# Sum passes by pairs of chunks, and the opening's loads issued inside the sort, in a four-layer graph network

## The chip, the cores and the metric

The kernel runs on one core of a Trainium2 chip. The metric is the device time of one execution in microseconds (us); less is better. The engines are named as in the profile: PE (TensorE, with PEld for its weight loads), DVE (VectorE), ACT (ScalarE), POOL (GpSimd) and SP (SyncE, which only issues DMAs).

## The reference, cut to what matters

There are 3125 nodes of 256 features and 100000 edges (`src`, `dst`), and four layers. Each layer has a graph part, a mixing part and experts. The change touches the graph sums of layers 1 and 2 and the ordering of edges in front of layer 0.

```python
# layer 1: mean over the edges of one source and one type, then a product with weights
index = row * N_EDGE_TYPE + edge_type              # row = src, col = dst, 7 types
sums = segment_sum(x[col], index)                  # 3125 * 7 segments
mean = sums / maximum(segment_sum(1, index), 1)
out  = mean.reshape(n, -1) @ weights
# layer 2: weighted sum over the edges of one destination
norm = dinv[row] * ew * dinv[col]
out  = segment_sum((x @ W)[row] * norm[:, None], col)
```

The kernel multiplies first and sums afterwards: for layer 1 it stores a table `rel_table` with a row of 256 numbers per node and type, and adds to each source node the rows of its edges, each weighted with one over the size of its run of equal source and type. For layer 2 the table `el` has one row per node, weighted with the edge weight.

## The kernel before, in words

**Order of the edges.** `order_edges` (line 2921) builds constants, stores a record of four numbers per edge (`store_records`), and sorts the edges twice, by destination (`order_by_dst`, line 508) and by source (`order_by_src`, line 451). Every stage is a `phase` (line 83): it has its own semaphores, and at its end all engines meet at a barrier. So a stage lasts as long as its last engine, SP's issuing included.

`order_by_dst` begins with the stage `dst_keys` (lines 518 to 537): SP issues the load of `dst`, then the loads in `ahead` (lines 522 and 523), which are the 17 weights, biases and gains that the opening of layer 0 reads and the two halves of x; GpSimd writes edge numbers and VectorE packs keys. `build_sort` (line 193) then sorts 128 x 1024 keys: exchanges on VectorE, with TensorE transposes and copies on ScalarE and VectorE from level 11 on; SP has nothing in it. `build_chunk_order` turns the keys to chunks of 128 edges. There are 784 chunks (CHUNKS_S), the last of them with padding.

`build_unit_tiles` (line 401) groups the chunks by G = 4 to 196 units and finds for each the tile of 125 nodes (25 tiles) in which its first node lies. Where a unit goes across the border of two tiles, its sum must reach both: so 24 further units are appended (UNITS_S = 220 in all, 880 chunks), each a copy of the unit at one border. The copies are made in a loop of 24 turns on VectorE: `value_load` of the position, then one copy for each name in `o["copied"]` (lines 440 to 444); line 447 subtracts each unit's first node. For the source order this is the stage `src_tiles`, for the destination order `dst_tiles`.

**Record gathers.** After the destination order is known, GpSimd fetches the 784 chunks' records by indirect DMAs (line 561), one per chunk. `SHARES` (line 41) divides them over the stages of the source order: 14 in `src_keys`, 280 in the sort, 40 in `runs`, 8 in `src_chunks`, 10 in `src_parts`, 36 in `src_tiles`, 16 in `src_out`, in which SP stores the source order to four DRAM arrays (node, row, w, tile) for layer 1. The other 380 are fetched in the opening of layer 0 (`open0`, line 1592), the first 128 of them paced. `unpack_records` (line 570) waits for all of them before layer 0 goes on.

**Sum passes.** `build_sums` (line 592) serves layer 1 (`layer1`, line 2966) and layer 2 (`layer2`, line 2975). For each of 220 units
- GpSimd gathers 4 chunks of 128 rows into one of 10 lanes (line 609), after the unit that had the lane is summed;
- VectorE makes four one-hot matrices (chunk edge by node of the tile, times the weight, line 622) in one of 14 buffers;
- TensorE multiplies the four with the rows into one PSUM slot of 16 (line 648). fp32 gives two PE instructions per matmul;
- VectorE loads the unit's tile to a register and adds the slot to the accumulator of that tile (line 631), BEHIND = 10 units after the one-hots.

TensorE signals once in BATCH = 4 units, on `batch_summed`. GpSimd's lanes, VectorE's one-hot buffers and VectorE's additions all wait on that semaphore:

```python
def batches_of(u):
    return u // BATCH + 1
# GpSimd, unit u, before its four gathers
if u >= LANES_S:
    pool.wait_ge(s["batch_summed"], batches_of(u - LANES_S))
```

TensorE waits for unit u on `step` u + 1, which VectorE raises after its one-hots of unit u and its addition of unit u - 10.

Of the kernel before, what the change touches and what calls it, by code (L numbers as in the profile page):

```python
# [6 lines left out]
F32 = mybir.dt.float32  # L7
# [25 lines left out]
LANES_S = 10  # L33
BATCH = 4
HOTS_S = 14
SLOTS_S = 16
BEHIND = 10
# [3 lines left out]
SHARES = (14, 280, 40, 8, 10, 36, 16)  # L41
# [151 lines left out]
def build_sort(nc, c, tag, T, turned, pool_work=None):  # L193
# [10 lines left out]
    with phase(nc, tag, "ready", "turned", "moved", "chain") as s, nc.Block() as block:  # L204
        @block.tensor
# [245 lines left out]
def order_by_src(nc, c, I, o, pool_works):  # L451
# [3 lines left out]
    o["copied"] = ("node", "row", "w")  # L455
    with ExitStack() as ctx:
# [48 lines left out]
        build_unit_tiles(nc, c, "src_tiles", o, pool_works[5])  # L505


def order_by_dst(nc, c, I, o, ahead):
# [4 lines left out]
    with ExitStack() as ctx:  # L513
# [24 lines left out]
        build_sort(nc, c, "dst_sort", T, turned)  # L538
# [48 lines left out]
def batches_of(u):  # L587

    return u // BATCH + 1


def build_sums(nc, c, tag, table, o, w, acc):

    assert UNITS_S % BATCH == 0 and HOTS_S >= BEHIND + BATCH and SLOTS_S >= BEHIND + BATCH and BATCH % 2 == 0
    with ExitStack() as ctx:
        rows = [ctx.enter_context(nc.sbuf_tensor(f"{tag}_rows{l}", [P, G, D], F32)) for l in range(LANES_S)]
        hot = [ctx.enter_context(nc.sbuf_tensor(f"{tag}_hot{l}", [P, G, R], F32)) for l in range(HOTS_S)]
        banks = [ctx.enter_context(nc.psum_tensor(f"{tag}_sum{l}", [R, 2, D], F32)) for l in range(SLOTS_S // 2)]
        slot = lambda u: banks[u % SLOTS_S // 2][:, u % 2, :]
        with phase(nc, tag, "cleared", "batch_summed", "step", *[f"rows_in{l}" for l in range(LANES_S)]) as s, nc.Block() as block:  # L600
            @block.gpsimd
            def _(pool):
                for u in range(UNITS_S):
# [3 lines left out]
                    for g in range(G):  # L607
                        k = u * G + g
                        nc.gpsimd.indirect_dma_start(rows[l][:, g, :], None, table, bass.IndirectOffsetOnAxis(ap=o["row"][:, k:k + 1], axis=0)  # L609
                                                     ).then_inc(s[f"rows_in{l}"], 16)  # L610

            @block.vector
            def _(dve):
                v = nc.vector
                v.memset(acc[:], 0.0).then_inc(s["cleared"], 1)

                def make_hot(u):
                    if u >= HOTS_S:
                        dve.wait_ge(s["batch_summed"], batches_of(u - HOTS_S))
                    for g in range(G):  # L620
                        k = u * G + g
                        last = v.tensor_scalar(hot[u % HOTS_S][:, g, :], c["iota"][:, 0:R], o["node"][:, k:k + 1], w[:, k:k + 1], ALU.is_equal, ALU.mult)
                    return last

                def add(u, steps):
                    at = dve.value_load(o["tile"][0:1, u:u + 1], min_val=0, max_val=TILES - 1)
                    to = acc[:, bass.ds(at, 1), :].rearrange("p t d -> p (t d)")
                    if u % BATCH == 0:
                        dve.wait_ge(s["batch_summed"], batches_of(u))
                    dve.wait_ge(s["step"], steps)  # L630
                    return v.tensor_tensor(to, to, slot(u), ALU.add)  # L631

                dve.wait_ge(s["cleared"], 1)
                for n in range(UNITS_S + BEHIND):
                    if n < UNITS_S:
                        last = make_hot(n)
                    if n >= BEHIND:
                        last = add(n - BEHIND, n)
                    last.then_inc(s["step"], 1)

            @block.tensor
            def _(pe):
                for u in range(UNITS_S):
                    l = u % LANES_S
                    pe.wait_ge(s["step"], u + 1)
                    pe.wait_ge(s[f"rows_in{l}"], 16 * G * (u // LANES_S + 1))
                    for g in range(G):
                        last = nc.tensor.matmul(slot(u), hot[u % HOTS_S][:, g, :], rows[l][:, g, :], start=(g == 0), stop=(g == G - 1))  # L648
                    if u % BATCH == BATCH - 1:
                        last.then_inc(s["batch_summed"], 1)  # L650
# [2262 lines left out]
def alloc_order(nc, ctx, by, names):  # L2913

    sb = lambda n, sh, d=F32: ctx.enter_context(nc.sbuf_tensor(f"{by}_order_{n}", sh, d))
    o = {n: sb(n, [P, COLS_S], I32 if n == "row" else F32) for n in names}
    o["tile"], o["again"] = sb("tile", [P, UNITS_S], I32), sb("again", [P, TILES], I32)
    return o


def order_edges(nc, c, I, by_src, by_dst, ahead):
# [4 lines left out]
    order_by_src(nc, c, I, by_src, [record_share(nc, by_dst, n) for n in range(6)])  # L2926
# [39 lines left out]
def layer1(nc, c, m, I, dram, by_src):  # L2966

    open1(nc, c, m, I, dram)
    with nc.sbuf_tensor("gnn1_acc", [R, TILES, D], F32) as acc:
        build_sums(nc, c, "sum1", dram["rel_table"], by_src, by_src["w"][:], acc)  # L2970
# [4 lines left out]
def layer2(nc, c, m, I, dram, by_dst):  # L2975

    with ExitStack() as ctx:
# [15 lines left out]
        with nc.sbuf_tensor("gnn2_acc", [R, TILES, D], F32) as acc:  # L2993
            build_sums(nc, c, "sum2", dram["el"], by_dst, by_dst["record"][:, :, 1], acc)
# [380 lines left out]
```

## Time and profile before

| what | us |
|---|---|
| median of the runs (lowest to highest) | 10286.64 (10276.81 to 10286.82) |
| the profiled execution, its own time | 10346.27 |
| its span, first to last instruction | 10344.1 |
| first sum pass, first to last gather | 3691.1 to 4935.2 |
| second sum pass, first to last gather | 5480.8 to 6724.9 |

The mean granted clock of TensorE is 0.80. In the profile a busy time is the time in which an engine works on instructions with data; register operations, such as those of `value_load`, semaphores and the issuing of DMAs are not in it. A row of the timeline has the start, the length, the engine, the line and what it writes and reads; in brackets stands how long the engine was idle before, and what is held to have ended that. The name of a releaser is inferred and can be wrong where several semaphores are waited for.

### The profile page before, as it was taken

What the parts mean: (1) busy time and instruction counts of PE and PEld (TensorE: products, weight loads), DVE (VectorE), ACT (ScalarE), POOL (GpSimd) and SP (SyncE); (2) the same over time, 40 slices, a digit from 0 to 9 for tenths busy, and PEclk for the clock granted to TensorE, in tenths of its full rate; (3) what the DMA queues carried; (4) which work ended last, traced back from release to release, by engine and by line L of the source; (5) the groups of instructions that cost most, each with busy time, mean ns of one, the idle gap of its engine ahead of it and who ended that gap; (6) DMA issues with size and microseconds to landing.
All of it is one profiled execution on the core that took longest, in us unless ns stands there. A gap on an engine that the chain in (4) does not pass through costs nothing. (4 is left out here: it accounts for less than half of the span.)

```text
span 10344.1 us, 95778 instructions
## 1 busy us (share of the span) xinstructions
PE 6288.6 (61%) x28050; PEld 4786.2 (46%) x28050; DVE 4856.2 (47%) x13537; ACT 2032.4 (20%) x5038; POOL 4487.0 (43%) x4412
## 2 busy tenths in 40 slices
PE   0001305999996864454754444553955788887699
PEld 0000204888874533333543333342853677775466
DVE  5644515888874632222242222274123566666633
ACT  0000102444442300000120000012212232222322
POOL 0375675666650046666005666602021666664000
PEclk9999657999997976666776666675987777777799
DMA  1000002333320133333002333302861232332000
GB/s 33 6 2 7 11 4 83 83 83 83 83 74 12 63 103 92 94 92 92 23 14 81 92 92 94 92 7 59 308 205 30 75 80 79 81 81 60 11 13 19
DMA packets 404431, 697.45 MB, mean 67 GB/s; under 512 B 154143, under 2 KB 267784, under 8 KB 403421
## 3 DMA queue, kind: packets, MB, share of 16 engines
q0 software_dynamic: 206848, 480.68, 17.2%
q1 hardware_dynamic: 197076, 210.68, 6.4%
q8 instruction: 236, 3.87, 0.2%
q14 instruction: 271, 2.22, 0.1%
HBM read 631.46 MB, written 59.47 MB: 67 GB/s over the span
## 5 line engine op out<-in xcount | busy, mean ns | idle before, releaser
L648 PE MATMUL sum_sum<-sum_rows,sum_hot 128*125 128x256 f32 x3520 | 1233.9, 489 | 1284.1 <-issue 802.1
L665 POOL DMA_INDIRECT att_rows<-el_table,dst_order_row x1520 | 1590.0, 1046 | 950.6 <-issue 388.4
L648 PEld LDWEIGHTS sum_sum<-sum_rows,sum_hot 128*125 128x125 f32 x3520 | 828.9, 241 | 1689.3 <-issue 1538.5
L609 POOL DMA_INDIRECT sum_rows<-rel_table,src_order_row x880 | 834.9, 949 | 1038.3 <-ACTq L600 628.2
L609 POOL DMA_INDIRECT sum_rows<-el_table,dst_order_row x880 | 834.7, 948 | 955.1 <-ACTq L600 544.7
L561 POOL DMA_INDIRECT dst_order_record<-records,dst_order_row x784 | 835.2, 1065 | 679.6 <-PEq L461 363.2
L631 DVE TENSOR_TENSOR gnn_acc<-gnn_acc,sum_sum 125x256 f32 x440 | 180.5, 410 | 1887.7 <-DMA ffn1e_w<-in_L_ffn_W_dram 938.6
L1143 PE MATMUL att_sum<-att_rows,att_hot 128*125 128x265 f32 x1280 | 426.8, 489 | 47.2 <-ACT att_part L1210 39.9
L665 POOL DMA_INDIRECT dst_order_record<-el_table,dst_order_row x240 | 268.5, 1119 | 407.2 <-SPq L967 241.7
L807 PE MATMUL att_found<-gnn_to_dst,att_hot_t 125*128 x1760 | 439.5, 393 | 2.5 <-ACT att_hot_t L856 2.5
L831 PE MATMUL att_sum<-att_rows,att_hot 128*125 128x261 f32 x1760 | 427.7, 385 | 2.4 <-ACT att_rows L869 2.4
L869 ACT ACTIVATE att_rows<-att_rows,att_p 128x257 f32<-128x257 f32 x880 | 375.7, 498 | 0.0
L797 PE MATMUL att_turn_p<-ident,att_hot 128*125 128x128 f32 x880 | 155.1, 299 | 328.0 <-DVE att_hot L675 315.4
L1143 PEld LDWEIGHTS att_sum<-att_rows,att_hot 128*125 128x125 f32 x1280 | 291.7, 240 | 126.4 <-issue 59.4
L1108 PEld LDWEIGHTS att_found<-layer_a_dst,att_hot_t 125*128 125x128 f32 x1760 | 275.0, 226 | 162.2 <-issue 141.0
L807 PEld LDWEIGHTS att_found<-gnn_to_dst,att_hot_t 125*128 125x128 f32 x1760 | 320.8, 192 | 38.4 <-issue 3.2
L831 PEld LDWEIGHTS att_sum<-att_rows,att_hot 128*125 128x125 f32 x1760 | 314.2, 188 | 47.8 <-ACT att_rows L869 2.5
L1108 PE MATMUL att_found<-layer_a_dst,att_hot_t 125*128 x1760 | 253.3, 267 | 122.9 <-issue 69.4
L751 DVE CUSTOM_DVE_ANT_0 att_high<-att_high,att_att 128x256 f32<-128x256 f32 x880 | 319.9, 418 | 0.0
L1169 ACT COPY att_hot_t<-att_turn_p 125x512 f32<-125x512 f32 x220 | 129.4, 588 | 793.2 <-PE att_turn_p L1098 447.8
L797 PEld LDWEIGHTS att_turn_p<-ident,att_hot 128*125 128x125 f32 x880 | 113.5, 188 | 369.8 <-DVE att_hot L675 367.2
L211 PE MATMUL src_order_turned<-ident,src_order_keys 128*128 128x128 f32 x112 | 27.6, 428 | 417.8 <-DVE src_order_keys L242 320.5
(775 smaller groups left out, 12991.9 us busy)
## 6 DMA issues: line engine op xcount, KB each, us to landing
block_w<-in_L_ffn_W_dram SPq DMA_DIRECT2D x112, 512.0 KB, 6.3
block_w<-in_L_ffn_W_dram SPq DMA_DIRECT2D x56, 1024.0 KB
att_rows<-el_table,dst_order_row POOLq DMA_INDIRECT x1520
rel_table<-open_st SPq DMA_DIRECT2D x25, 784.0 KB
sum_rows<-rel_table,src_order_row POOLq DMA_INDIRECT x880
sum_rows<-el_table,dst_order_row POOLq DMA_INDIRECT x880
dst_order_record<-records,dst_order_row POOLq DMA_INDIRECT x784
pairs<-zeros SPq DMA_DIRECT2D x1, 7168.0 KB
```

Of the source, the lines that this page charges most:

```text
L561: nc.gpsimd.indirect_dma_start(o["record"][:, k, :], None, o["records"], bass.IndirectOffsetOnAxis(ap=o["row"][:, k:k + 1], axis=0)).then_ ...
L609: nc.gpsimd.indirect_dma_start(rows[l][:, g, :], None, table, bass.IndirectOffsetOnAxis(ap=o["row"][:, k:k + 1], axis=0)).then_inc(s[f"row ...
L631: return v.tensor_tensor(to, to, slot(u), ALU.add)
L648: last = nc.tensor.matmul(slot(u), hot[u % HOTS_S][:, g, :], rows[l][:, g, :], start=(g == 0), stop=(g == G - 1))
L665: nc.gpsimd.indirect_dma_start(rows[l][:, g, 0:width], None, table, bass.IndirectOffsetOnAxis(ap=o["row"][:, k:k + 1], axis=0)).then_inc(s ...
L751: last = v.tensor_tensor_reduce(high[:, g, :], high[:, g, :], att[:], 0.8, 0.0, ALU.mult, ALU.add, score[u % 2][:, g:g + 1])
L797: last = t.transpose(turn_p[:, g * P:(g + 1) * P], hot[u % HOTS][:, g, :], c["ident"][:])
L807: last = t.matmul(found[:, g, :], hot_t[u % TURNED][:, g * P:(g + 1) * P], nodes_of_unit(to_dst, tile), start=True, stop=True)
L831: last = t.matmul(sums[u % 2][:, 0:S], hot[u % HOTS][:, g, :], rows[u % LANES_A][:, g, :], start=(g == 0), stop=(g == G - 1))
L869: last = a.activation(own_rows[:, g, 0:D + 1], own_rows[:, g, 0:D + 1], ACT.Copy, scale=p[u % 2][:, g:g + 1])
L1108: done = t.matmul(found[u % 2][:, g, 0:H], hot_t[u % 2][:, g * P:(g + 1) * P], nodes_of_unit(to_dst, tile), start=True, stop=True)
L1143: done = t.matmul(sums[u % SUMS_B][:, 0:W + 1], hot[u % HOTS_B][:, g, :], rows[u % LANES_B][:, g, :], start=(g == 0), stop=(g == G - 1))
```

## The change

The constants: LANES_S 10 to 9, HOTS_S 14 to 10, BEHIND 10 to 6, BATCH goes; HALF_S = 2, MAIN_S = 782, EXTRA_S = 48, SUM_COLS = 830, SUM_UNITS = 208, SUMS_S = 415. SHARES becomes (14, 280, 40, 8, 10, 8): 360 gathers before the opening of layer 0 and 424 in it.

In the sum passes a sum and a tile now belong to two chunks (HALF_S), 415 of them; at each of the 24 borders two chunks are repeated instead of four. Of 784 chunks 782 are used: 100000 edges fill 781.25. Rows are still gathered, one-hot made and multiplied by units of four chunks, 208 of them. TensorE signals each unit (`summed`), VectorE its one-hots (`hot`) and each addition (`added`). The tiles and the repeated chunks are now worked out at the head of each pass (`prepare_sums`), from the plain order; the stage `src_tiles` goes, and the fourth store and load (tile) with it. `dst_tiles` remains, since layers 0 and 3 use its units; for layer 2 node numbers are rebuilt from it.

```diff
-def build_sort(nc, c, tag, T, turned, pool_work=None):
+def build_sort(nc, c, tag, T, turned, pool_work=None, ahead=None):
...
+        @block.sync
+        def _(sp):
+            if ahead:
+                for to, frm in ahead[1]:
+                    sp.dma_start(to, frm).then_inc(ahead[0], 16)
@@ order_by_src
-        build_unit_tiles(nc, c, "src_tiles", o, pool_works[5])
@@ order_by_dst
                 sp.dma_start(dst_i[:], as_chunks(I["dst"])).then_inc(s["loaded"], 16)
-                for to, frm in ahead[1]:
-                    sp.dma_start(to, frm).then_inc(ahead[0], 16)
...
-        build_sort(nc, c, "dst_sort", T, turned)
+        build_sort(nc, c, "dst_sort", T, turned, ahead=ahead)
@@ new, called first by VectorE's part of build_sums
+def prepare_sums(nc, c, dve, pe_done, to_pe, own, b, node, tile_of, row, w):
...
+    if tile_of is None:
+        own(v.tensor_copy(b["node"][:, main], node[:, main]))
+    else:
+        own(v.tensor_copy(b["tile"][:, 0:UNITS_1], tile_of[:, 0:UNITS_1]))
+        own(v.scalar_tensor_tensor(b["node"][:, 0:CHUNKS_S]..., col_of(b["tile"][:, 0:UNITS_1], G), float(R), node[:, 0:CHUNKS_S]..., ALU.mult, ALU.add))
+    own(v.tensor_copy(b["w"][:, main], w[:, main]))
+    v.tensor_copy(b["tile"][:, extras], c["iota"][:, 1:TILES]).then_inc(to_pe, 1)
+    dve.wait_ge(pe_done, 1)
+    own(v.tensor_scalar(b["tile"][:, halves], b["first_p"][:, 0:MAIN_S // HALF_S], -62.0, 1.0 / R, ALU.add, ALU.mult))
+    own(v.tensor_scalar(b["tile"][:, halves], b["tile"][:, halves], 8388608.0 * 1.5, -8388608.0 * 1.5, ALU.add, ALU.add))
+    own(v.tensor_scalar(b["less"], b["tile"][0:R, halves], c["part"][0:R], 0.5, ALU.subtract, ALU.is_lt))
+    own(v.tensor_reduce(b["cnt"][:], b["less"], AX, ALU.add))
...
+    for k in range(TILES - 1):
+        at = dve.value_load(b["again"][0:1, k:k + 1], min_val=0, max_val=MAIN_S - HALF_S)
+        to = MAIN_S + k * HALF_S
+        v.tensor_copy(b["node"][:, to:to + HALF_S], b["node"][:, bass.ds(at, HALF_S)])
+        v.tensor_copy(b["w"][:, to:to + HALF_S], b["w"][:, bass.ds(at, HALF_S)])
+        last = v.tensor_copy(b["row"][:, to - MAIN_S:to - MAIN_S + HALF_S], row[:, bass.ds(at, HALF_S)])
+    own(last)
+    own(v.tensor_tensor(b["node"]..., b["node"]..., col_of(b["tile"][:], HALF_S), ALU.subtract))
@@ build_sums, GpSimd
+                for u in range(SUM_UNITS):
                     l = u % LANES_S
                     if u >= LANES_S:
-                        pool.wait_ge(s["batch_summed"], batches_of(u - LANES_S))
+                        pool.wait_ge(s["summed"], u - LANES_S + 1)
...
+                            if k == MAIN_S:
+                                pool.wait_ge(s["cleared"], 1)
@@ build_sums, VectorE
+                prepare_sums(nc, c, dve, s["firsts"], s["ready"], own, b, node, tile_of, row, w)
                 v.memset(acc[:], 0.0).then_inc(s["cleared"], 1)
...
                     if u >= HOTS_S:
-                        dve.wait_ge(s["batch_summed"], batches_of(u - HOTS_S))
+                        dve.wait_ge(s["summed"], u - HOTS_S + 1)
...
+                    last.then_inc(s["hot"], 1)
+                def add(u):
+                    for h in range(u * G // HALF_S, ends(u)):
+                        at = dve.value_load(b["tile_i"][0:1, h:h + 1], min_val=0, max_val=TILES - 1)
+                        to = acc[:, bass.ds(at, 1), :].rearrange("p t d -> p (t d)")
+                        if h == u * G // HALF_S:
+                            dve.wait_ge(s["summed"], u + 1)
+                        if h:
+                            dve.wait_ge(s["added"], h)
+                        v.tensor_tensor(to, to, slot(h), ALU.add).then_inc(s["added"], 1)
@@ build_sums, TensorE
+                pe.wait_ge(s["ready"], 1)
...
+                last.then_inc(s["firsts"], 1)
+                pe.wait_ge(s["ready"], 2)
+                nc.tensor.matmul(b["again_p"], c["ones"][0:R, :], b["spread"][:], start=True, stop=True).then_inc(s["firsts"], 1)
+                for u in range(SUM_UNITS):
                     l = u % LANES_S
-                    pe.wait_ge(s["step"], u + 1)
+                    pe.wait_ge(s["hot"], u + 1)
+                    if u >= slots_ahead:
+                        pe.wait_ge(s["added"], ends(u - slots_ahead))
...
+                    for k in chunks(u):
+                        last = nc.tensor.matmul(slot(k // HALF_S), hot[u % HOTS_S][:, k % G, :], rows[l][:, k % G, :], start=(k % HALF_S == 0), stop=(k % HALF_S == HALF_S - 1))
+                    last.then_inc(s["summed"], 1)
```

The tables in DRAM and the source order's arrays get 784 columns instead of 880.

## Rows read from the trace of the kernel before

**Rows 1.** The page: its first line, and part 1 (busy us, share, instructions).

```profile
span 10344.1 us, 95778 instructions
...
PE 6288.6 (61%) x28050; PEld 4786.2 (46%) x28050; DVE 4856.2 (47%) x13537; ACT 2032.4 (20%) x5038; POOL 4487.0 (43%) x4412
...
```

**Rows 2.** Timeline of the opening: start, us, engine, line, idle before.

```profile
...
37.03 0.36 SPq L523 DMA_DIRECT2D open_w_el<-in_L_gnn_W_src_dram  x1
...
43.45 0.99 DVE L537 TENSOR_TENSOR dst_order_keys<-dst_order_dst_i,dst_order_edge_i 125x800 int32<-125x800 int32 x1
...
83.53 26.42 SPq L523 DMA_DIRECT2D X<-in_x_dram  x2
...
110.89 0.43 DVE L253 TENSOR_SCALAR dst_order_keys<-dst_order_keys 128x512 f32<-128x512 f32 x1 [66.45 <-PEq L88]
...
```

**Rows 3.** Timeline of VectorE in the source order's last stages.

```profile
...
905.32 0.97 DVE L503 SCALAR_TENSOR_TENSOR src_order_typ<-src_order_dst,src_order_typ 128x784 f32<-128x784 f32 x1
...
931.75 0.17 DVE L444 COPY src_order_node<-src_order_node 128x4 f32 x1 [0.77 <-DVE src_order_tile L439]
...
938.99 0.17 DVE L444 COPY src_order_node<-src_order_node 128x4 f32 x1 [0.78 <-issue]
...
969.30 0.17 DVE L444 COPY src_order_node<-src_order_node 128x4 f32 x1 [3.41 <-issue]
...
980.32 0.17 DVE L444 COPY src_order_node<-src_order_node 128x4 f32 x1 [0.56 <-issue]
...
980.74 1.07 DVE L447 TENSOR_TENSOR src_order_node<-src_order_node,src_tiles_base 128x880 f32<-128x880 f32 x1
```

**Rows 4.** Timeline of GpSimd there: record gathers at the ends of stages.

```profile
...
913.67 0.94 POOL L561 DMA_INDIRECT dst_order_record<-records,dst_order_row  x1 [0.30 <-issue]
917.69 0.94 POOL L561 DMA_INDIRECT dst_order_record<-records,dst_order_row  x1 [3.08 <-SPq L412]
...
983.35 0.95 POOL L561 DMA_INDIRECT dst_order_record<-records,dst_order_row  x1 [17.09 <-PEq L2132]
...
1006.44 0.95 POOL L561 DMA_INDIRECT dst_order_record<-records,dst_order_row  x1 [3.38 <-POOLq L88]
...
```

**Rows 5.** Line 561, then windows: length, busy of PE, PEld, DVE, ACT, POOL, clock.

```profile
...
L561 POOL DMA_INDIRECT dst_order_record<-records,dst_order_row x784: 940/947/4741, 400.8 to 1588.5; - x196
...
1350.00:1500.00 150.00, 0.00 (x0) 0.00 (x0) 0.00 (x0) 0.00 (x0) 113.42 (x121) 0.50 0.05 2
1500.00:1590.00 90.00, 0.00 (x0) 0.00 (x0) 0.00 (x0) 0.00 (x0) 68.22 (x71) 0.50 0.05 2
...
```

**Rows 6.** Line 609 in both passes; then groups of lines in the first pass.

```profile
...
L609 POOL DMA_INDIRECT sum_rows<-rel_table,src_order_row x880: 942/947/1050, 3691.1 to 4935.2; - x176
...
L609 POOL DMA_INDIRECT sum_rows<-rel_table,src_order_row x880 | 834.9, 949 | 1038.3 <-ACTq L600 628.2 <-issue 260.0 <-DMA ffn0e_w<-in_L_ffn_eW_dram 150.1
...
```

**Rows 7.** Timeline of GpSimd in the first sum pass, around two pauses.

```profile
...
3808.63 0.95 POOL L609 DMA_INDIRECT sum_rows<-rel_table,src_order_row  x1 [0.30 <-issue]
3815.17 0.95 POOL L609 DMA_INDIRECT sum_rows<-rel_table,src_order_row  x1 [5.59 <-DMA ffn0e_w<-in_L_ffn_eW_dram]
...
3860.63 0.95 POOL L609 DMA_INDIRECT sum_rows<-rel_table,src_order_row  x1 [5.66 <-DMA ffn0e_w<-in_L_ffn_eW_dram]
...
```

**Rows 8.** Timeline of TensorE and VectorE around the first of them.

```profile
...
3809.93 0.59 PE L648 MATMUL sum_sum<-sum_rows,sum_hot 128*125 128x256 f32 x1 [2.21 <-issue]
...
3812.03 0.59 PE L648 MATMUL sum_sum<-sum_rows,sum_hot 128*125 128x256 f32 x1 [1.51 <-issue]
...
3813.43 11.46 PE L648 MATMUL sum_sum<-sum_rows,sum_hot 128*125 128x256 f32 x38 [0.81 <-issue]
...
3815.04 0.42 DVE L631 TENSOR_TENSOR gnn_acc<-gnn_acc,sum_sum 125x256 f32 x1 [33.90 <-DMA ffn0e_w<-in_L_ffn_eW_dram]
...
```

**Rows 9.** Timeline of VectorE at the start and the end of that pass.

```profile
...
3691.86 5.39 DVE L615 MEMSET gnn_acc<- 125x6400 f32 x1 [2.30 <-issue]
...
4948.42 0.42 DVE L631 TENSOR_TENSOR gnn_acc<-gnn_acc,sum_sum 125x256 f32 x1 [0.34 <-DVE gnn_acc L631]
...
```

More of the change, by code:

```diff
@@ new lines, in build_sums @@
+def build_sums(nc, c, tag, table, node, tile_of, row, w, acc):
+    chunks = lambda u: range(u * G, min((u + 1) * G, SUM_COLS))
+    ends = lambda u: (u * G + len(chunks(u))) // HALF_S
+    slots_ahead = SLOTS_S * HALF_S // G
+    assert HOTS_S > BEHIND and G % HALF_S == 0 and SUM_COLS % HALF_S == 0
+    with ExitStack() as ctx:
+        sb = lambda n, sh, d=F32: ctx.enter_context(nc.sbuf_tensor(f"{tag}_{n}", sh, d))
+        rows = [sb(f"rows{l}", [P, G, D]) for l in range(LANES_S)]
+        hot = [sb(f"hot{l}", [P, G, R]) for l in range(HOTS_S)]
+        b = {"node": sb("node", [P, SUM_COLS]), "w": sb("w", [P, SUM_COLS]), "row": sb("row", [P, EXTRA_S], I32), "tile": sb("tile", [P, SUMS_S]),
+             "tile_i": sb("tile_i", [P, SUMS_S], I32), "less": acc[:].rearrange("p t d -> p (t d)")[:, 0:MAIN_S // HALF_S], "cnt": sb("cnt", [R, 1]), "none": sb("none", [R, 1]),
+             "spread": sb("spread", [R, 2, TILES - 1]), "again": sb("again", [P, TILES - 1], I32)}
+        sums = ctx.enter_context(nc.psum_tensor(f"{tag}_sum", [P, SLOTS_S, D], F32))
+        slot = lambda h: sums[0:R, h % SLOTS_S, :]
+        halves = MAIN_S // HALF_S
+        b["first_p"], b["again_p"] = sums[:, 0:4, :].rearrange("p s d -> p (s d)"), sums[:, 4, 0:2 * (TILES - 1)].rearrange("p (k t) -> p k t", k=2)
+        with phase(nc, tag, "ready", "firsts", "cleared", "chain", "hot", "added", "summed", *[f"rows_in{l}" for l in range(LANES_S)]) as s, nc.Block() as block:
@@ L614, in _ @@
                 v = nc.vector
+                own = Chain(dve, s["chain"])
+                prepare_sums(nc, c, dve, s["firsts"], s["ready"], own, b, node, tile_of, row, w)
                 v.memset(acc[:], 0.0).then_inc(s["cleared"], 1)
@@ new lines, in make_hot @@
+                    for k in chunks(u):
+                        last = v.tensor_scalar(hot[u % HOTS_S][:, k % G, :], c["iota"][:, 0:R], b["node"][:, k:k + 1], b["w"][:, k:k + 1], ALU.is_equal, ALU.mult)
+                    last.then_inc(s["hot"], 1)
[8 more added lines that the diff above has]
+                        v.tensor_tensor(to, to, slot(h), ALU.add).then_inc(s["added"], 1)
@@ L633, in _ @@
                 dve.wait_ge(s["cleared"], 1)
-                for n in range(UNITS_S + BEHIND):
-                    if n < UNITS_S:
-                        last = make_hot(n)
+                for n in range(SUM_UNITS + BEHIND):
+                    if n < SUM_UNITS:
+                        make_hot(n)
                     if n >= BEHIND:
-                        last = add(n - BEHIND, n)
-                    last.then_inc(s["step"], 1)
+                        add(n - BEHIND)
             @block.tensor
@@ L642, in _ @@
             def _(pe):
-                for u in range(UNITS_S):
-                    l = u % LANES_S
-                    pe.wait_ge(s["step"], u + 1)
[L646 to L650, printed above, removed]
+                firsts = b["node"][:, 0:MAIN_S].rearrange("p (u g) -> p u g", g=HALF_S)[:, :, 0]
@@ L2925, in order_edges @@
     order_by_dst(nc, c, I, by_dst, ahead)
-    order_by_src(nc, c, I, by_src, [record_share(nc, by_dst, n) for n in range(6)])
+    order_by_src(nc, c, I, by_src, [record_share(nc, by_dst, n) for n in range(5)])
 def as_chunks(v):
@@ L2993, in layer2 @@
         with nc.sbuf_tensor("gnn2_acc", [R, TILES, D], F32) as acc:
-            build_sums(nc, c, "sum2", dram["el"], by_dst, by_dst["record"][:, :, 1], acc)
+            build_sums(nc, c, "sum2", dram["el"], by_dst["node"][:], by_dst["tile"][:], by_dst["row"][:], by_dst["record"][:, :, 1], acc)
             close2(nc, c, m, I, acc)
@@ L3323, in build @@
             "pairs": scratch("pairs", [BLOCKS * P, D]), "results": scratch("results", [BLOCKS * P, D])}
-    dram |= {"src_" + n: scratch("src_order_of_" + n, [P, UNITS_S if n == "tile" else COLS_S], I32 if n in ("row", "tile") else F32) for n in ("node", "row", "w", "tile")}
+    dram |= {"src_" + n: scratch("src_order_of_" + n, [P, CHUNKS_S], I32 if n == "row" else F32) for n in ("node", "row", "w")}
     with ExitStack() as ctx:
@@ L3345, in build @@
         with ExitStack() as again:
[L3346 to L3347 removed]
+            by_src = alloc_order(nc, again, "src1", ("node", "row", "w"), CHUNKS_S)
+            experts0(nc, c, m, I, [(by_src[n][:], dram["src_" + n]) for n in ("node", "row", "w")])
             layer1(nc, c, m, I, dram, by_src)
```

82 lines of the change are left out of this document (42 added, 40 removed).

## The prediction

> **What bounds the kernel now.** I read the page first, then the stages that the diff touches. The page shows no engine above 61% of the span [rows 1], so the price of each edit has to be read in its own stage. The diff touches three.
>
> The opening's order stages are chains. In the first one VectorE ends its last instruction at 43.45 + 0.99 = 44.44 us and does nothing until 110.89 us, because the stage ends only when SP has issued the 19 loads of line 523 (37.03 to 83.53 + 26.42 = 109.95 us) [rows 2]. In the building of tiles for the source order, GpSimd ends its 36 record gathers at 966.3 us and waits 17.09 us for VectorE's loop of 24 turns [rows 3, 4]. After that GpSimd is the bound: all 784 record gathers have to be done before layer 0, and from 1350 to 1590 us the other engines are idle while it makes 192 of them [rows 5].
>
> In each sum pass GpSimd issues 880 gathers in 1244.1 us (3691.1 to 4935.2) [rows 6]. A gather takes 0.95 us and a gap of 0.30, but every 32 gathers there is a pause of 5.6 to 5.7 us; 26 pauses make 150.1 us [rows 6, 7]. So 8 units take 45.46 us (3815.17 to 3860.63), 5.68 us a unit and 1.42 us a gather. What ends a pause is not the load named in the row, long landed; I read it from the code: unit 22 may overwrite lane 2 only when batch 4 (units 12 to 15) is summed, and VectorE, which waits for the same batch, resumes at 3815.04, GpSimd at 3815.17 [rows 7, 8]. TensorE's array isn't slow by itself: while gathers run, it starts one matmul in about 2.1 to 2.8 us; 4.8 us after the last gather before the pause it bursts, 38 in 11.5 us [rows 7, 8]. VectorE shows the same thing in rows 3: the first 8 turns of its loop start 1.03 us apart (931.75 to 938.99), the next 6 while GpSimd gathers 5.05 us apart (to 969.30), the last 10 some 1.1 us apart (to 980.32), when it has stopped. So under dense gathers another engine's stream runs slowly after a while, and GpSimd has to pause for it to catch up. This share, 5.68 - 5.01 = 0.67 us a unit, is what the changed loop can alter; the other 5.01 us only falls with the number of gathers.
>
> **Part 1, loads moved into the sort.** The sort can start when VectorE is done: 44.44 + 0.94 (from SP's end at 109.95 to VectorE's start at 110.89) = 45.4 us [rows 2]. That is 65.5 us earlier, and every later stage of the opening hangs on it. The 19 issues go to SP inside the sort, where it has nothing else; they take 73 us and are hidden by a stage that lasts to about 400 us, since the first record gather is at 400.8 [rows 5]. Their data is wanted in the opening of layer 0, at 1006 us. If that cover were gone the whole 65.5 us would come back. Bounds: 0 to 65.5; I take 65.5, as the sort's chain has no instruction on SP.
>
> **Part 2, no tile stage for the source order.** It disappears with 36 gathers in it, and 8 of the 16 in the stage of the stores go too; these 44 are issued at the end. Before: from the gather at 913.67 to the last at 1588.46. Now: the stores' stage starts its 8 gathers at 917.7, issues the last at 926.5, and the next stage begins 4.3 us later (0.95 + 3.38) [rows 4], at 930.8. Its first 380 gathers take 582.0 us as now (1006.44 to 1588.46), the 44 more cost 55 us at the pace of the empty stretch, 240 / 192 = 1.25 us [rows 5]. End 1567.8, a gain of 20.7 us. The three stores hide behind the 8 gathers; should they not, 10 us are lost. Bounds 10 to 30.
>
> **Part 3, the sum passes.** 830 gathers (782 + 48) instead of 880.
> Preparation: VectorE now computes tiles and copies 24 x 3 pieces inside the pass, ahead of its first one-hot. Some 12 us of copies and small operations come first (up to 0.97 us each, as the one of 784 columns in rows 3), then the loop. GpSimd fills its 9 lanes with 36 gathers in 45 us and then waits for the first sum. The loop, priced by rows 3: 8 turns at 1.03 us to 20 us, then 5.05 us a turn, 6 turns until the gathers stop counting at 50 us (4.8 us after the last, as above), the last 10 at 1.0 us. With 1.07 us for the subtraction, 5.39 us for the memset [rows 3, 9] and about 4 us of one-hots and matmuls, GpSimd goes on at 70 us: 25 us lost in each pass. Bounds: 0 (all turns at 1.03 us) to 40.
> Steady part: 9 lanes released unit by unit allow TensorE to be 8 units behind; before it was 6 to 9, because a batch of four is released at once, and the worst case set the pause. But VectorE now has two loads of a tile and two additions per unit, an addition taking 0.42 + 0.34 = 0.76 us when they follow each other [rows 9]. Four one-hots and two additions are some 2.2 us of 5, no bound by themselves. The two changes have opposite signs and neither has a row; I leave the pace at 1.42 us. Bounds: the 0.67 us halved or increased by half, which is 67 us in a pass either way.
> Pass: 45 + 25 + 794 x 1.421 + 13.7 (last gather 4935.2 to 4948.8) [rows 9] = 1212 us against 1244.1 + 13.7 = 1258. That is -46, and -92 for both. One of four loads for layer 1 goes as well, beside the experts. The other new pieces (two small matmuls, three semaphores, a wait of GpSimd before gather 782 for something done 1100 us earlier) lie beside gathers and cost nothing.
>
> Sum: -65.5 - 20.7 - 92 = -178 us. The profiled execution took 10346.3 us, its span 10344.1; it becomes 10168. It lies 59.6 us above the median of the runs, 10286.64, which I carry over: 10109, so **10110 us**.
>
> One rule deserves weighing. The rows show engines slowed under gathers, but in a recorded execution only [rows 3, 8]. The Trainium skill, "NOTIFIC — the notification-queue block", section 7.1, says that the block which writes trace records pushes back inside rather than lose a record, and that such a stall can throttle an engine. By it the pauses might not exist in unrecorded runs; then each pass gains 50 x 1.2525 = 63 us, and the whole is -65 - 8 - 125 = -198, or 10089. Against it: 52 pauses are worth 300 us, and the recorded execution is only 59.6 us longer. I give it 0.07.
>
> **Rivals.**
> B, the pauses vanish: unit-wise release lets GpSimd run through. A pass is 830 x 1.2525 + 25 + 13.7 = 1078, -180 each; total -446, 9840 us. For it: the pause follows a batch. Against it: TensorE falls behind as long as gathers flow, and only a pause lets it catch up [rows 8], so more slack delays the pause and does not abolish it. 0.12.
> C, slower: VectorE's stream in the sum loop. It has twice the loads and additions of before, and rows 3 show what such a loop becomes under gathers. If the 0.67 us doubles, a unit takes 6.35 us, a pass 84 + 794 x 1.5875 = 1344, +87 each; total +87, 10373 us. It decides from 6.13 us a unit on, where the passes eat the 86 us of parts 1 and 2. Against it: the pause relieves all engines at once, and VectorE now idles 34 of 45 us. 0.06.
> D, the sort runs beside the loads and is slowed by them, so that part 1 brings nothing: 10175 us. 0.05.
> E, the costs of C just about eat the gain: within 0.2%. 0.03.
>
> **How the numbers follow.** My case has 0.67, with 10040 to 10190 as its own range (a quarter of the 0.67 us either way, 10 us of part 2, 15 us of preparation per pass). The range 10000 to 10220 adds D, the skill's case and most of part 3's bounds, and leaves out B and C, 0.18. About 0.2% is what a measurement of this kernel can tell from no change. Faster by more 0.91, within it 0.03, slower 0.06.
>
> **What would show it.** The first exchange of the sort at about 45 us; the last record gather near 1502 us (1588 - 65 - 21); 830 gathers per pass with pauses still there, 40 to 50 us apart, and one pause of some 25 us after the 36th. A pass of 1079 us proves B, above 1300 C. If the first sort step isn't at 45 us, part 1 is wrong; if the first pause is missing, the preparation was mis-sized.

## The result, and the profile after

The changed kernel takes 10131.01 us (median of 4 runs, 10127.85 to 10144.78) against 10286.73 us of the kernel before on the same chip (4 runs): ratio 0.9848, 95% interval 0.9831 to 0.9866, 156 us less. In two later groups of runs, each with its own runs of the kernel before, the same pair gave 0.9832 (0.9806 to 0.9858), 184 us, and 0.9847 (0.9830 to 0.9865), 163 us. The forecast was 10110, which is 178 less than the median before, rounded.

The profiled execution took 10133.58 us. Its page, first line and part 1, against [rows 1]:

```profile
span 10131.8 us, 97631 instructions
...
PE 6172.4 (61%) x27856; PEld 4734.8 (47%) x27856; DVE 5008.2 (49%) x13919; ACT 2035.5 (20%) x5038; POOL 4420.1 (44%) x4312
```

No share tells where the time went; the starts of the same work in both traces do:

| start of | before | after | difference |
|---|---|---|---|
| first step of the sort | 110.89 | 44.55 | -66.3 |
| last record gather | 1588.5 | 1506.0 | -82.5 |
| first gather of the first sum pass | 3691.1 | 3607.5 | -83.6 |
| its last gather | 4935.2 | 4806.2 | -129.0 |
| first gather of the second pass | 5480.8 | 5353.1 | -127.7 |
| its last gather | 6724.9 | 6550.8 | -174.1 |
| first gather of layer 3 | 7980.2 | 7800.9 | -179.3 |
| last gather of layer 3 | 9480.5 | 9264.1 | -216.4 |

Up to layer 3 the difference is the predicted 178. The last 37 us come from a stage that the change does not touch; the repeated runs below deal with it. (The ends of the spans differ by 212.3 us, the medians by 156: the record of before lies 59.6 us above its median, that of after 2.6.) Timeline of the opening of the changed kernel, the answer to [rows 2]: VectorE's sort begins 0.94 us after its keys, and SP's loads (now line 214) run beside it.

```profile
42.62 0.99 DVE L544 TENSOR_TENSOR dst_order_keys<-dst_order_dst_i,dst_order_edge_i 125x800 int32<-125x800 int32 x1
44.50 0.36 SPq L214 DMA_DIRECT2D open_w_el<-in_L_gnn_W_src_dram  x1
...
44.55 0.43 DVE L264 TENSOR_SCALAR dst_order_keys<-dst_order_keys 128x512 f32<-128x512 f32 x1 [0.94 <-PEq L93]
```

The gathers of both passes and of the records, by line (count, ns, first and last start), against [rows 5, 6]: a pass is 1198.7 and 1197.7 us long where it was 1244.1.

```profile
L661 POOL DMA_INDIRECT sum_rows<-rel_table,src_order_row x782: 942/949/1126, 3607.5 to 4736.2; - x196
L661 POOL DMA_INDIRECT sum_rows<-el_table,dst_order_row x782: 942/949/1670, 5353.1 to 6481.4; - x196
L661 POOL DMA_INDIRECT sum_rows<-rel_table,sum_row x48: 942/948/1067, 4737.4 to 4806.2; - x48
L661 POOL DMA_INDIRECT sum_rows<-el_table,sum_row x48: 942/949/1043, 6482.7 to 6550.8; - x48
```

```profile
L568 POOL DMA_INDIRECT dst_order_record<-records,dst_order_row x784: 939/947/3532, 334.4 to 1506.0; - x196
```

The head of the first pass on VectorE. The first turn of the copy loop is at 3615.29; two turns while GpSimd gathers stand 7.7 us apart; the one-hots begin at 3677.14.

```profile
3606.91 0.57 DVE L600 COPY sum_node<-src_order_node 128x782 f32<-128x782 f32 x1 [0.93 <-PEq L93]
...
3615.29 0.17 DVE L623 COPY sum_node<-sum_node 128x2 f32 x1 [0.78 <-DVE sum_tile L619]
...
3647.49 0.17 DVE L623 COPY sum_node<-sum_node 128x2 f32 x1 [5.43 <-issue]
...
3655.20 0.17 DVE L623 COPY sum_node<-sum_node 128x2 f32 x1 [4.70 <-issue]
...
3669.28 1.02 DVE L627 TENSOR_TENSOR sum_node<-sum_node,sum_tile 128x830 f32<-128x830 f32 x1
3671.71 5.39 DVE L669 MEMSET gnn_acc<- 125x6400 f32 x1 [1.40 <-issue]
3677.14 7.22 DVE L675 TENSOR_SCALAR sum_hot<-iota,sum_node,sum_w 128x125 f32<-128x125 f32 x28
```

GpSimd beside it: after its 36th gather it waits 29.48 us. In the steady part (here of the second pass) runs of 28 gathers are the most frequent, each followed by a wait such as the 4.83 us shown, where it waited 5.6 after 32 [rows 7]: 28 take 5774.06 - 5734.25 = 39.8 us, 1.42 a gather, as before. Shorter runs, mostly of 24 and of 4, stand between them, so that the two passes have 38 and 30 pauses beside the long wait, where each had 26.

```profile
3651.55 0.95 POOL L661 DMA_INDIRECT sum_rows<-rel_table,src_order_row  x1 [0.30 <-issue]
3681.98 0.97 POOL L661 DMA_INDIRECT sum_rows<-rel_table,src_order_row  x1 [29.48 <-PE sum_sum L711]
```

```profile
5768.28 0.95 POOL L661 DMA_INDIRECT sum_rows<-el_table,dst_order_row  x1 [0.30 <-issue]
5774.06 0.94 POOL L661 DMA_INDIRECT sum_rows<-el_table,dst_order_row  x1 [4.83 <-DMA sum_rows<-rel_table,sum_row]
```

One thing the rows ahead of the prediction do not show, because they average it away. In the stretch of the opening in which no other engine works, the record gathers are 1.25 us apart up to 1419.34, and 1.40 from 1420.59 on, because the gather itself takes 1.10 us instead of 0.94. The kernel before does the same, but only in its last 11 gathers, from 1574.47 on. After, then before:

```profile
1419.34 0.94 POOL L568 DMA_INDIRECT dst_order_record<-records,dst_order_row  x1 [0.31 <-issue]
1420.59 1.10 POOL L568 DMA_INDIRECT dst_order_record<-records,dst_order_row  x1 [0.30 <-issue]
```

```profile
1573.21 0.95 POOL L561 DMA_INDIRECT dst_order_record<-records,dst_order_row  x1 [0.30 <-issue]
1574.47 1.09 POOL L561 DMA_INDIRECT dst_order_record<-records,dst_order_row  x1 [0.30 <-issue]
```

### The profile page after: what moved, and what is told of

The parts are those of the page before. It is cut to its first block and busy times, and to the rows that moved or that the text cites. A ratio compares the mean times of both kernels' runs of the same rounds, so it can differ in the third digit from the quotient of the medians.

```text
span 10131.8 us, 97631 instructions
## 1 busy us (share of the span) xinstructions
PE 6172.4 (61%) x27856; PEld 4734.8 (47%) x27856; DVE 5008.2 (49%) x13919; ACT 2035.5 (20%) x5038; POOL 4420.1 (44%) x4312
## 5 line engine op out<-in xcount | busy, mean ns | idle before, releaser
L711 PE MATMUL sum_sum<-sum_rows,sum_hot 128*125 128x256 f32 x3320 | 1111.5, 465 | 1295.4 <-issue 1132.1
L711 PEld LDWEIGHTS sum_sum<-sum_rows,sum_hot 128*125 128x125 f32 x3320 | 762.8, 231 | 1643.7 <-issue 1388.2
L661 POOL DMA_INDIRECT sum_rows<-rel_table,src_order_row x782 | 745.7, 954 | 1009.5 <-ACTq L647 625.7
L661 POOL DMA_INDIRECT sum_rows<-el_table,dst_order_row x782 | 746.6, 955 | 928.7 <-ACTq L647 545.9
L686 DVE TENSOR_TENSOR gnn_acc<-gnn_acc,sum_sum 125x256 f32 x830 | 347.3, 418 | 1533.4 <-remote 632.2
L675 DVE TENSOR_SCALAR sum_hot<-iota,sum_node,sum_w 128x125 f32<-128x125 f32 x1660 | 470.4, 358 | 0.1
```

Source lines behind the costliest of these rows:

```text
L661: nc.gpsimd.indirect_dma_start(rows[l][:, k % G, :], None, table, bass.IndirectOffsetOnAxis(ap=at, axis=0)).then_inc(s[f"rows_in{l}"], 16)
L675: last = v.tensor_scalar(hot[u % HOTS_S][:, k % G, :], c["iota"][:, 0:R], b["node"][:, k:k + 1], b["w"][:, k:k + 1], ALU.is_equal, ALU.mult)
L686: v.tensor_tensor(to, to, slot(h), ALU.add).then_inc(s["added"], 1)
L711: last = nc.tensor.matmul(slot(k // HALF_S), hot[u % HOTS_S][:, k % G, :], rows[l][:, k % G, :], start=(k % HALF_S == 0), stop=(k % HALF_S ...
```

## The experiments

"Excess" is what the pauses take beyond the pitch of 1.25 us, summed over a pass and divided by its gathers. A pause is where two gathers start 2.5 us or more apart; the one long wait for the preparation is not in it. It is 0.162 us in before and 0.15 in after. All spans of a pass are from first to last gather.

**Part 1 alone.** In the kernel before, the diff's loop over `ahead[1]` is moved from `dst_keys` to SP's part of the first sort, and nothing else.

> The kernel before, with the opening's loads alone moved from the key stage into the first sort. If the loads' issuing was what the sort waited for, and nothing else of the sort is touched, the sort starts at 45 us instead of 110.9 and the whole is 66 us shorter than before: about 10221 us, with both sum passes still at 1244 us from first to last gather. If the sort running beside the loads gives some of it back (rival D), the time lies between 10225 and 10287 us.

10272.59 us against 10337.12 of before in that group of runs, ratio 0.9939 (0.9917 to 0.9962), 64.5 us less. The sort starts at 44.58, layer 0's gathers 66.2 us earlier than in before's record, and the passes keep 1244.7 and 1245.0 us. Part 1 is as predicted; rival D falls.

**The repeats made later.**

```diff
-    for k in range(TILES - 1): (24 turns, before the memset)
+    # in the loop of the units, after add(n - BEHIND)
+    k = n - 12
+    if 0 <= k < TILES - 1:
+        last = repeat(dve, v, b, base, w, row, k)
...
-                            if k == MAIN_S: pool.wait_ge(s["cleared"], 1)
+                            if k == MAIN_S: pool.wait_ge(s["repeated"], 1)
```

> The changed kernel, but the 24 turns that copy the repeated chunks are taken out of the head of the pass: VectorE makes one of them after each of the units 12 to 35, the one-hots begin right after the tiles, and GpSimd waits for the repeats only before gather 782. If the pause of 29.5 us after gather 36 is the price of those 24 turns alone, it vanishes; the steady pace of 1.42 us a gather then holds for all 830: 830 x 1.42 = 1178 us from first to last gather instead of 1199, 20 us less in each pass, about 10090 us. Rival: the turns are as dear among the gathers (5 us each while the streams are slow, and VectorE then holds back the sums); then pauses of the same sum appear between units 12 and 36 and the time stays within 10 us of 10131.

Passes of 1180.9 and 1179.8 us, 18 less than in after, ratio to before 0.9813 (0.9787 to 0.9838). The wait of 29.5 us is the price of the 24 turns, as expected; a wait of 7.5 us comes in its place after 48 gathers, and the excess is 0.165. The median is 10128.30 us, where 10090 was expected; the kernel before has 10337 here and not 10287.

**More lanes, fewer lanes.** `LANES_S` 11 (with `HOTS_S` 7), 6 and 4 in place of 9. The first two ran together, the last one later.

> The changed kernel with 11 lanes for the gathered rows instead of 9 (7 one-hot buffers instead of 10, to make room). Theory F, a pause has a fixed length: each costs 4.5 us beyond the pitch, and a run between two has 4 x (lanes - 2) gathers (28 in the changed kernel's trace), so with 11 lanes runs of 36, 0.125 us a gather instead of 0.16, about 30 us less in each pass, 10070 us in all. Theory G, a debt: other engines lose a fixed share of work for each gather and the pause must pay it back; then longer runs are followed by longer pauses (5.8 us beyond the pitch after 36), the excess stays 0.16 us a gather, and the time stays within 10 us of 10131.

> The changed kernel with 6 lanes instead of 9. Theory F (fixed pause of 4.5 us beyond the pitch after runs of 4 x (lanes - 2) = 16 gathers): 0.28 us a gather more than the bare 1.2525, a pass of about 1298 us from first to last gather, 100 us more in each, about 10330 us. Theory G (debt paid back in proportion to the gathers): runs of 16 with pauses of 2.6 us beyond the pitch, the same 1.42 us a gather, a pass within 15 us of 1199, about 10140 us.

> The changed kernel with 4 lanes. A run can't be longer than about 16 gathers while TensorE is behind. If a pause has a least length (the 4 to 5 us after the last gather in which the others are still slow), the excess rises towards 4.5 us in 16 gathers, 0.28 us a gather, and a pass takes some 1290 us, 90 more than 1199. If short runs leave no debt, because the slow time begins only some 13 us after the gathers start again, the pauses get shorter with them and a pass stays within 20 us of 1199.

Passes of 1203.2 and 1203.2 us with 11 lanes, 1206.1 and 1204.6 with 6, 1205.1 and 1202.6 with 4; excess 0.154 to 0.157, 0.156, 0.147. The ratios to before are 0.9860, 0.9843 and 0.9842, where the changed kernel had 0.9848. Runs of 24 to 28 gathers are the most frequent with each number of lanes, so the lanes don't set their length either. The pause goes with the run before it: with 4 lanes 2.2 us after 12 gathers, 3.0 after 24 and 3.8 after 28 (means, beyond the pitch), and 5.4 after 32 in the kernel before. Theory F falls. G holds in its number: whatever the lanes, GpSimd rests about 0.15 us for each gather. It doesn't say why.

**Less work in one stream.** Only the first chunk of each pair multiplied (`chunks(u)[::HALF_S]`); then, separately, only the first of a unit's two additions made.

> The changed kernel with the products of every second chunk left out in the sum passes: TensorE has 9 entries a unit (4 weight loads, 4 matmuls, a wait) instead of 17; gathers, one-hots and additions stay. The 6 and the 11 lanes left the excess at 0.15 to 0.16 us a gather, with runs of 24 to 28 gathers whatever the lanes. Theory P: TensorE's entries set it, so many run fast after each rest and few while gathers flow; with half of them a run gets about twice as long, the excess falls to 0.08 us a gather or below, a pass is at most 1135 us from first to last gather instead of 1199, the whole at least 125 us shorter than the changed kernel. Theory V: VectorE's entries (15 a unit) set it; then nothing changes beyond 10 us a pass.

> The changed kernel with every second addition (and its load of a tile) left out in the sum passes: VectorE has about 10 entries a unit instead of 15, nearly the 9 of before; TensorE keeps its 17. Theory P (TensorE's entries set the pauses): the excess stays 0.15 us a gather, the pass within 10 us of 1199. Theory V (VectorE's do): the excess falls by a third, 0.10 us a gather, about 40 us less in each pass, 80 us in all.

Passes of 1196.0 and 1203.2 us, and of 1196.2 and 1195.3; excess 0.148 and 0.154, 0.148 and 0.144. The ratios to before are 0.9867 and 0.9823, that of the changed kernel beside them 0.9832. Neither P nor V: halving either stream leaves the mean pace where it was.

**A quarter of the work in both streams.** One one-hot, one product, one addition a unit.

> The changed kernel with most of the work around the gathers left out: in each unit one one-hot, one product and one addition instead of four, four and two (TensorE 5 entries a unit instead of 17, VectorE about 7 instead of 15). All 830 gathers stay. Halving one stream at a time changed nothing (0.148 to 0.154 us a gather). If the slower of two streams sets the pauses, so that each hid behind the other, the excess now falls to a half or less, below 0.075 us a gather, and a pass to below 1140 us. If the pause is owed for each gather, whatever the others do (GpSimd, its DMAs and their signals), the excess stays between 0.13 and 0.17 and a pass within 20 us of 1198.

Between the two: passes of 1182.0 and 1182.8 us, excess 0.115 and 0.125; ratio to before 0.9824. The form of the pass explained more than the sum. GpSimd made 292 gathers after the preparation with no wait above 0.8 us: the first 173 of them 1.25 us apart, the later ones about 1.40. Then it fell into a locked stretch in which a unit takes 7.00 us and GpSimd waits 2.3 us before each unit. Timeline of VectorE, and of GpSimd, in it:

```profile
4080.60 0.42 DVE L686 TENSOR_TENSOR gnn_acc<-gnn_acc,sum_sum 125x256 f32 x1 [6.33 <-issue]
...
4087.59 0.42 DVE L686 TENSOR_TENSOR gnn_acc<-gnn_acc,sum_sum 125x256 f32 x1 [6.31 <-issue]
```

```profile
4082.82 0.95 POOL L661 DMA_INDIRECT sum_rows<-rel_table,src_order_row  x1 [2.30 <-issue]
...
4089.82 0.95 POOL L661 DMA_INDIRECT sum_rows<-rel_table,src_order_row  x1 [2.28 <-issue]
```

"Issue" means that VectorE waited for nothing that the timeline shows. The trace's list of all instructions has what it did: the wait, load, register and assert entries between two additions stand 0.70 or 1.40 us apart. Among the gathers after the long wait, up to 3709 us, nearly all of the same entries take 0.02 to 0.31 us.

**The same without the loads of a tile.** `to = acc[:, h * TILES // SUMS_S, :]` in place of the loaded tile, so that VectorE has no register entry left.

> As the kernel with a quarter of the work, but each addition goes to a tile fixed in the program, so that VectorE has no load of a tile to a register: 3 entries a unit (one-hot, wait, addition) instead of 7, TensorE 5 as there. That kernel's trace shows 292 gathers without a pause and then a locked stretch in which a unit takes 7.00 us and every register or wait entry of VectorE stands 0.70 or 1.40 us apart, where it takes 0.02 to 0.31 otherwise: 7 entries in 7.0 us, about 1 us each. Theory T (a toll on each entry of the other engines' streams while gathers flow): with 3 and 5 entries a unit needs at most 5 us, as long as its four gathers take, so the pauses vanish: excess below 0.03 us a gather and a pass of 45 + 28 + 794 x 1.26 = 1074 us from first to last gather, against 1182. Theory D (each gather leaves a debt that GpSimd has to wait out, whatever the others' entries): the excess stays above 0.10 and the pass within 15 us of 1182.

Neither theory is right whole. There is no pause at all after the preparation, and the other streams stay on time, as T said; but a pass takes 1155.4 and 1155.2 us, not 1074 (median 10043.48 us, ratio to before 0.9756). GpSimd's own gathers slow down. Timeline of GpSimd in it, and windows of 200 us (busy us and count of each engine, POOL the fifth):

```profile
4006.11 1.00 POOL L661 DMA_INDIRECT sum_rows<-rel_table,src_order_row  x1 [0.30 <-issue]
4007.41 0.95 POOL L661 DMA_INDIRECT sum_rows<-rel_table,src_order_row  x1 [0.30 <-remote]
4008.67 1.24 POOL L661 DMA_INDIRECT sum_rows<-rel_table,src_order_row  x1 [0.30 <-issue]
4010.21 1.80 POOL L661 DMA_INDIRECT sum_rows<-rel_table,src_order_row  x1 [0.30 <-issue]
```

```profile
3676.00:3876.00 200.00, 49.75 (x92) 22.04 (x90) 31.71 (x94) 0.00 (x0) 151.27 (x161) 0.52 0.37 105
3876.00:4076.00 200.00, 42.75 (x72) 17.81 (x72) 24.48 (x72) 0.00 (x0) 155.84 (x146) 0.50 0.33 95
4076.00:4276.00 200.00, 42.75 (x72) 17.80 (x72) 23.85 (x71) 0.00 (x0) 156.67 (x143) 0.50 0.33 94
```

The first 177 gathers after the wait are 1.25 us apart; from 3896.67 on, every eight take 11.20 us (two of them 1.24 and 1.80), and it stays so to the end: 143 in 200 us, **1.40 us a gather**. The record gathers of before and after show the same 1.40 in a stretch in which no engine but GpSimd does anything; such gathers move 2 GB/s [rows 5], these 94.

**The repeats made by ScalarE.** As the late repeats, but ScalarE, idle in a pass, makes the 24 turns; VectorE only casts the row numbers and subtracts the tiles at unit 150.

> As the kernel with the late repeats, but the 24 turns are made by ScalarE, which has nothing else to do in a pass, beside the sums; VectorE only casts the row numbers and subtracts the tiles once, at unit 150. The late repeats on VectorE took 1180 us a pass, 18 less than the changed kernel, with shorter runs (20 to 24 gathers) while the turns were made. If it was the turns' entries on VectorE that shortened those runs, a pass is now 1198 - 29 + 36 x 0.15 = 1175 us, 5 less than with late repeats and 24 less than the changed kernel; both passes 48 us. If the debt goes by gathers alone, the pass stays at 1180 (36 us less in both).

Passes of 1184.1 and 1184.3 us, excess 0.167 and 0.166. They are 22 and 21 us shorter than those of the changed kernel run beside it (1206.1 and 1205.1), 43 of the 48 us between the medians, 10111.35 and 10159.25 us. That lies between the two readings, 24 and 18, and the late turns on VectorE were measured in another group, so whether their entries cost anything is not settled. Ratio to before 0.9807 (0.9787 to 0.9828), where the changed kernel in the same group has 0.9847 (0.9830 to 0.9865): the intervals lie side by side. It is the lowest ratio of a version that leaves nothing out, and not told apart from the 0.9813 of the late turns on VectorE. About 29 us a pass of waiting are gone and 22 are gained, since a pause comes due earlier.

**The changed kernel again**, in two groups of runs.

> The changed kernel itself, once more, beside the runs of before on the same chip. The records of before and after agree with the predicted sum (178 us) up to 8200 us of the span, and differ by a further 34 us in the gathers of layer 3, which the change doesn't touch. If that is a matter of the chip and the execution, layer 3 comes out differently here with the same kernel, and the time saved lies between 155 and 200 us. If it is a lasting effect of the change (memory placed elsewhere), layer 3 is again 34 us shorter than in before's record.

> The changed kernel once more, for comparison on the same chip: sum passes of 1198 us from first to last gather (1197.1 to 1198.8 in the four passes recorded so far), and 150 to 190 us less than before.

184 and 163 us less than before; passes of 1197.1 and 1198.8, and of 1206.1 and 1205.1 us. Layer 3, from its first to its last gather, took 1500.3 us in the record of before, 1499.1 with the loads moved alone, 1463.2 in after, 1458.9 and 1480.3 in these two. It goes with the group of runs: where before had a median of 10277 to 10287 us, the records of changed kernels have 1454 to 1464; where it had 10322 or 10337, 1476 to 1493. Whether that is the chip is not known, since the record gives the last two groups the same chip number. So a good part of the last 37 us between the two records is no effect of the change; but the two records with the loops of before, 1500.3 and 1499.1, are the longest of all, and some 7 to 23 us may be an effect of it. That was not separated. One more difference between records of one kernel: the first gather of layer 0 came at 1554.8, 1524.3 and 1530.6 us.

## Why the prediction was right, and where its reason was not

**Part 1**, -65.5: shown, -66.3 in the trace, -64.5 in the timed run by itself. The loads cost the sort nothing.

**Part 2**, -20.7: 82.5 - 66.3 = 16.2 us up to the last record gather. The prediction priced the 44 more gathers of the empty stretch at 1.25 us, the mean of [rows 5]. The last 62 (1420.59 to 1505.99) took 1.40 where before had 11 such, and the 51 more cost 7.6 us, which covers the missing 4.5. The two other records of the kernel have none of them; they end at 1491.0 and 1497.3, a gain of 31 and 25 us. So the term was met within what two records of one kernel differ by, and no better.

**Part 3, preparation**, 25 us lost and GpSimd on again 70 us after the pass begins: 29.5 and 74.5. The small operations ahead of the loop took 8 us instead of 12 (3606.91 to 3615.29); the 24 turns took 54 instead of 48, up to 7.7 us apiece among gathers where [rows 3] have 5.05. The late repeats show that this wait is theirs.

**Part 3, steady pace**, 1.42 us a gather kept: right, 1198.7 against the 1198 of the sum, with some luck, since 4.5 us more of waiting for the preparation met 4 us less in the 794 gathers behind it. The pauses came more often than the 40 to 50 us that were named as a sign: some 40 us apart at most, many of them less. The pass's tail is 16.6 us (4806.17 to 4822.82) where 13.7 was put. So the sum of 178 stands in the records at 179 before layer 3, and the medians gave 156, 184 and 163.

**The reason for the pace is the step that failed.** The prediction read the pauses as the time in which TensorE and VectorE catch up, took 5.01 us a unit as the floor and the other 0.67 us as "what the changed loop can alter", and bounded it at 67 us a pass either way. The kept traces contradict the first, the runs the second.

What GpSimd waited for was long done. The gathers of unit 22 wait for units 12 to 15 [rows 7]. These are the eight PE instructions of unit 15, the 121st to 128th of the pass, in the trace of before:

```profile
3781.44 1.96 PE L648 MATMUL sum_sum<-sum_rows,sum_hot 128*125 128x256 f32 x8 [1.22 <-DMA sum_rows<-rel_table,src_order_row]
```

They end at 3783.4, 26 us before the pause begins (3809.58). The semaphore update that ends the wait is recorded at 3814.91, and VectorE and GpSimd go on at 3815.04 and 3815.17. At all 26 pauses of that pass GpSimd goes on 26 to 32 us after the sum that it waits for has ended; in after it is 31 us (median), with 6 lanes 24, with 4 lanes 14. After the long wait for the preparation it is 0.27 us. So in a pause the sum is done and its signal comes late. TensorE does fall behind under dense gathers, as the prediction read it (unit 17 takes from 3791.44 to 3807.72), but with units that nobody waits for at that pause. Only where work was left out is it otherwise: a median of 5 us with half the matmuls, and 0.27 us in the locked stretch, where GpSimd really waits for TensorE.

The floor is another one too: 1.40 us a gather in the long run, 5.60 a unit, with no pause at all. With lanes from 4 to 11, half the products, half the additions, the pace behind the long wait is 1.41 to 1.43. What the pauses cost is mostly what the gathers would cost anyway in the long run: 28 x 0.15 = 4.2 of the 4.5 us. Of the 0.67 us only 0.08 (5.68 - 5.60) could be had in the long run, some 17 us a pass. The kernel without a pause gained more, 40 us in the 794 gathers behind the long wait, because its first 177 still went at 1.25 us. That the lanes, the unit-wise release and the doubled additions left the pace alone was therefore no balance of opposite signs, as the text had it. That one limit lies behind both the pauses and the 1.40 us is what the equal paces suggest; it is not shown.

**Rival B** is a pass of 1078 us with its tail of 13.7, or 1065 from first to last gather, without pauses. It was not merely unlikely: with no pause a pass took 1155 us, 91 more. **Rival C** asked for an entry on VectorE to be dear under gathers, which the locked stretch of the quarter-work kernel shows (7.00 us a unit); with the full kernel's pauses it never set the pace: half the additions gave nothing.

**The rule of the Trainium skill** ("NOTIFIC — the notification-queue block", section 7.1, that the block pushes back inside rather than lose a record, and that such a stall can throttle an engine) might have made the pauses absent from unrecorded runs. Every timed run here carries a span, so none shows what an unrecorded one does, and the rule is neither shown nor excluded. A limit on the number of instruction records alone does not give the pace: counted in the traces, there are 6.3 of them a us in the first pass of after, 2.1 in the pass without pauses and 0.7 in the slow end of the empty stretch, with 1.42, 1.40 and 1.40 us a gather. In its price of this case the prediction has 8 us for part 2, where its own sum has 20.7, and does not say why.

**What stays open.** Which resource takes 1.40 us for a gather, and whether it is the one that makes signals late and other engines' entries slow, was not found. Three things speak for a common queue. 177 gathers at 0.15 us put GpSimd 27 us ahead of it before a gather gets longer. Signals are late by such times (with 4 lanes, the sum of a unit ended at 3925.5 and GpSimd, which waited for it, went on at 3940.8, after its rest). And in all 14 records the wait between the last record gather and layer 0 goes with it: it is 48.6 to 48.9 us in the nine in which the gathers had reached the 1.40, before among them, and 33.3 in the five in which they had not. Against it speak those five, where 252 to 255 record gathers go at 1.25 us up to the last. This was argued, not shown.

## What to carry to other kernels

Before pricing a wait as recoverable, look when the thing waited for was done: here that was 26 us before the pause began, so the partner's lag was not what the pause was for. Then find the long-run rate of the engine that waits, in a stretch long enough to have it: here 192 gathers in 240 us looked like a rate of 1.25 us, and only the last 11 of them had reached the 1.40. Where an engine's pauses keep a constant price for each of its operations while lanes, batches and the partners' work change, expect only fewer operations to help: 50 fewer gathers are worth 71 us a pass, and the preparation took 25 of them back. A loop of register loads is best kept away from the head of a stage in which another engine fills its buffers.

## What was not expected of the hardware

A chain of indirect gathers of 128 rows on GpSimd goes at 1.25 us at first and then at 1.40 us, with rows of 1 KB (94 GB/s) and with records of four numbers alike. How many go at 1.25 differs: 177 and 181 in the two passes without pauses, 185 to 205 in the openings of nine records, and all 252 to 255 in those of five others. Two executions of the same kernel differ by 30 us at the start of layer 0 (1554.8 and 1524.3), 15 of it between the last record gather and that start (48.8 and 33.3 us); the first had reached the 1.40, the second had not, and so it is in every record. What decides which of the two an execution does was not found. A signal of TensorE can reach VectorE and GpSimd some 31 us after its last matmul has ended (3783.4 and 3814.91). And in a dense stretch the register and wait entries of VectorE can stand 0.70 or 1.40 us apart, with the engine itself idle, where they otherwise take 0.02 to 0.31.
